# Self attention stage: one group of query-key products, operations moved off VectorE, input rows stored in halves, steps written out

## What is computed

```python
phi_q = relu(q) + 0.001;  phi_k = relu(k) + 0.001
kv  = cumsum(einsum('bshm,bshd->bshmd', phi_k, v), axis=1)
num = einsum('bshm,bshmd->bshd', phi_q, kv)
den = einsum('bshm,bshm->bsh', phi_q, cumsum(phi_k, axis=1))
attn = num / den[..., None]                       # 16 heads of 32
# block:  x1 = x + xattn(x);  u = layernorm(x1);  y = layernorm(u) * s1 + b1
#         q, k, v = y @ w_qkv;  xm = attn @ wo2 + u;  z = layernorm(xm) * s2 + b2
#         out = x1 + z + xm + gelu(z @ w1 + b1) @ w2 + b2
```

## Time and profile before

| what | value |
|---|---|
| median of 3 runs | 3508.2 us |
| profiled execution, first to last instruction | 3505.6 us |
| TensorE busy | 3440.8 us, 98% |
| VectorE busy | 1766.6 us, 50% |
| ScalarE busy | 1110.5 us, 32% |
| GpSimd busy | 2032.7 us, 58% |
| mean granted TensorE clock | 0.997 |
| self attention stage, `y` transposes of steps 2 to 16 | 2396.47 to 2690.32 us |

### The profile page before, as it was taken

How to read it: one execution, slowest core, us unless ns; L and a number is a source line. 1 busy time by engine, 2 the same in 40 slices (tenths; PEclk the granted TensorE clock), 3 DMA queues, 4 the chain that set the end, 5 groups by cost and what they waited for, 6 DMA issues and landing times.

```text
span 3505.6 us, 77874 instructions
## 1 busy us (share of the span) xinstructions
PE 3440.8 (98%) x32204; PEld 2683.7 (77%) x32204; DVE 1766.6 (50%) x3285; ACT 1110.5 (32%) x1284; POOL 2032.7 (58%) x1175
## 2 busy tenths in 40 slices
PE   7999999999999999999999999999999999999999
PEld 6777777777777777777777777777777788878887
DVE  6523333233332333333323333256888688789997
ACT  2233333333333333333333333342112422321111
POOL 3177867778677787786777867733444400123332
PEclk9999999999999999999999999999999999999999
DMA  4111110110110101111011011021112432320000
GB/s 139 58 43 35 37 35 31 41 47 28 38 40 25 47 28 44 34 37 35 29 44 36 35 35 45 27 89 41 49 51 78 136 99 99 126 67 25 24 18 19
DMA packets 83371, 174.64 MB, mean 50 GB/s; under 512 B 7184, under 2 KB 43152, under 8 KB 73872
## 3 DMA queue, kind: packets, MB, share of 16 engines
q1 hardware_dynamic: 83088, 170.24, 14.3%
HBM read 136.39 MB, written 33.82 MB: 49 GB/s over the span
## 4 chain that ended last, share of the span: by engine, by line
PE 89%; DVE 7%; issue 2%; ACT 1%; DMA 1%; POOL 1%; SPq 0%; DVEq 0%; ACTq 0%; POOLq 0%
PE a_bank L92 64%; PE a_bank L1294 8%; PE a_bank L1321 7%; PE a_bank L1309 6%; PE a_bank L1304 2%; DVE s_rden L604 1%; DVE s_am L546 1%; PE a_bank L2280 0%; PE a_bank L1340 0%; ACT x_probsT L1077 0%; DMA m_ff_src<-in_w_ff 0%; DVE m_hT L1753 0%; DVE s_yT L577 0%; PE a_bank L763 0%; DVE s_st L104 0%
## 5 line engine op out<-in xcount | busy, mean ns | idle before, releaser
L1155 DVE TENSOR_REDUCE x_maxima<-a_bank 128x1 f32<-128x512 f32 x960 | 593.4, 683 | 1226.1 <-PE a_bank L1294 1226.1
L92 PE MATMUL a_bank<-x_wv,x_ctx 128*128 128x512 f32 x3072 | 745.3, 396 | 1.1 <-ACT q_out L204 1.1
L894 POOL TENSOR_TENSOR x_pairs<-x_probsT 128x1024 f32<-128x1024 f32 x240 | 572.8, 2387 | 297.0 <-ACT x_probsT L1069 297.0
L92 PE MATMUL a_bank<-x_ctx,x_wk 128*128 128x512 f32 x3072 | 742.4, 396 | 0.0
L92 PEld LDWEIGHTS a_bank<-x_wv,x_ctx 128*128 128x128 f32 x3072 | 563.8, 188 | 166.5 <-DVE x_maxima L1155 27.3
L92 PEld LDWEIGHTS a_bank<-x_ctx,x_wk 128*128 128x128 f32 x3072 | 564.7, 188 | 135.7 <-issue 11.9
L1069 ACT ACTIVATE x_probsT<-a_bank 128x2048 f32<-128x2048 f32 x240 | 451.7, 1882 | 329.1 <-PE a_bank L1309 329.1
L1062 ACT ACTIVATE x_v<-a_bank 128x512 f32<-128x512 f32 x256 | 152.9, 597 | 611.8 <-PE a_bank L92 611.8
L1058 ACT ACTIVATE x_k<-a_bank,x_bk 128x512 f32<-128x512 f32 x256 | 176.2, 688 | 481.6 <-PE a_bank L92 481.6
L1002 POOL TENSOR_TENSOR x_ctx<-x_ctx_raw,x_ctx 128x2048 fp32r<-128x2048 f32 x64 | 294.7, 4604 | 5.0
L1294 PE MATMUL a_bank<-x_k,x_q_max 32*128 32x512 f32 x2048 | 283.5, 633 | 0.0
(11 more groups left out here) (207 smaller groups left out, 3987.1 us busy)
## 6 DMA issues: line engine op xcount, KB each, us to landing
x_ctx_raw<-in_ctx SPq DMA_DIRECT2D x64, 1024.0 KB, 5.0
m_ff_src<-in_w_ff SPq DMA_DIRECT2D x44, 192.0 KB, 2.5
wq_ff<-m_ff_dst SPq DMA_DIRECT2D x44, 192.0 KB, 1.8
m_w_raw<-in_w SPq DMA_DIRECT2D x32, 256.0 KB, 2.8
f_w_in<-wq_ff SPq DMA_DIRECT2D x22, 256.0 KB, 3.4
q_x<-in_x SPq DMA_DIRECT2D x16, 256.0 KB, 4.4
q_all<-q_out SPq DMA_DIRECT2D x16, 256.0 KB, 2.2
x_q_max<-q_all SPq DMA_DIRECT2D x16, 256.0 KB, 7.1
```

The costliest lines, as they stand in the source:

```text
L92: mm = pe.matmul(out, lhs[a], rhs[b], start=first and n == 0, stop=last and n == 2)
L894: eng.tensor_tensor(pairs[:], probs(i, s)[:, :, 0:2], probs(i, s)[:, :, 2:4], ALU.add).then_inc(paired, 1)
L1155: dve.tensor_reduce(maxima[:, c, g * HG + j:g * HG + j + 1], banks[:, j], AX.X, ALU.max).then_inc(maxed, 1)
```

## The change

- The query-key products of all four strips are issued in one call, at the place of the second call before, and masked by two operations of 1024 columns instead of four of 512.
- `attT` in device memory holds two halves. GpSimd makes them after the bias (two operations more per item), the store moves 512 KB and not 256, the stage loads them straight into the matmul's operand, and `input_hi` and `input_lo` are gone.
- `phi_q` and `kT` move from VectorE to ScalarE, where 0.001 is added after the transposition. The residual is computed on GpSimd as `xm + x1`; the sum `xu` is gone.
- Statistics are BN_STATS, BN_AGGR and one small addition.
- VectorE's list is reordered: reciprocal first, then the low half of `yT`, `an`, `x1`, the low half of `an`, `u`, the masks, `yn`, `xm` and `zn`.
- `normalise_last` and the bias behind it move from step 2 to the end of step 5, the store to step 6.
- All steps on all engines are written out; there is no hardware loop in the stage.

```diff
+STAT_LINKS = 2
+def row_stats(dve, src, st, eps, chain, before, var_ready):
+    dve.bn_stats(st[:, 0:6], src).then_inc(chain, 1)
+    dve.wait_ge(chain, before + 1)
+    dve.bn_aggr(st[:, 8:10], st[:, 0:6]).then_inc(chain, 1)
+    dve.wait_ge(chain, before + 2)
+    dve.tensor_scalar(st[:, 10:11], st[:, 9:10], eps, None, ALU.add).then_inc(var_ready, 1)
...
+def written_out(step, depth, first=0):
+    for n in range(first, B + depth):
+        step(Tile(n // UNROLL, n % UNROLL))
...
-        await_count(sp, attT_lo, s.count(plus=-1))
-        sp.dma_start(att_t[:, s.ring(2)], att_v[s.n][s.k]).then_inc(att_loaded[s.ring(2)], 16)
+        await_count(sp, m1, s.count(plus=-1))
+        sp.dma_start(attT[s.ring(2)][:].bitcast(F32), att_v[s.n][s.k]).then_inc(att_loaded[s.ring(2)], 16)
...
-            if nth(s, 2):
+            if s.count() == LAST_AT + 1:
...
-            if add_last_bias and nth(s, 2):
-                add_last_bias()
             rsqrt(pool, 0, s)
-            pool.wait_ge(u_ready, START + s.count(plus=1))
-            pool.tensor_tensor(xu[s.k][:], x1[:], u[s.k][:], ALU.add).then_inc(xu_ready, 1)
...
+            pool.wait_ge(xm_ready, START + e.count(plus=1))
+            await_count(pool, r_stored[e.ring(2)], e.back(e.ring(2)).count(8))
+            pool.tensor_tensor(r_out[:, e.ring(2)], xm[:], x1[e.k][:], ALU.add).then_inc(r_ready, 1)
...
+        if add_last_bias and s.count() == LAST_AT:
+            add_last_bias()
...
+            act.wait_ge(qkv, START + e.count(3, 1))
+            act.activation(phi_q[:], bank[0], ACT.Relu).then_inc(q_ready, 1)
...
-            act.activation(qT[:], bank[5], ACT.Copy).then_inc(qT_ready, 1)
-            if drain(s) == 0:
-                act.wait_ge(set_up, START + 4)
-                act.wait_ge(t3, START + e.count(2, 2))
-                act.activation(kT[:], bank[6], ACT.Identity, bias=eps_t[:]).then_inc(kT_ready, 1)
+            act.activation(qT[:], bank[5], ACT.Identity, bias=eps_t[:]).then_inc(qT_ready, 1)
+            act.wait_ge(t3, START + e.count(2, 2))
+            act.activation(kT[:], bank[6], ACT.Identity, bias=eps_t[:]).then_inc(kT_ready, 1)
...
+    def mask_products(dve, e):
+        dve.wait_ge(a_done, START + e.count(plus=1))
+        mask = causal[:].rearrange("p (g s) -> p g s", g=1).to_broadcast([P, 2 * DC, S])
+        for j in range(0, HG, 2):
+            dve.tensor_tensor(am[:, j:j + 2].rearrange("p j g s -> p (j g) s"),
+                              banks[:, 2 + j:4 + j].rearrange("p j (g s) -> p (j g) s", g=DC), mask,
+                              ALU.mult).then_inc(am_ready, 1)
...
+        await_count(dve, r_ready, e.count())
         dve.wait_ge(m3, START + e.count(plus=1))
         dve.tensor_tensor(xm[:], bank[2], u[e.k][:], ALU.add).then_inc(xm_ready, 1)
-        dve.wait_ge(xu_ready, START + e.count(plus=1))
-        await_count(dve, r_stored[e.ring(2)], e.back(e.ring(2)).count(8))
-        dve.tensor_tensor(r_out[:, e.ring(2)], bank[2], xu[e.k][:], ALU.add).then_inc(r_ready, 1)
...
+    def invert(dve, e):
+        dve.wait_ge(nd, START + e.count(plus=1))
+        dve.reciprocal(rden[:], bank[4]).then_inc(rden_ready, 1)
+    def scale_attention(dve, e):
+        dve.wait_ge(rden_ready, START + e.count(plus=1))
+        await_count(dve, anT_lo, e.count())
+        dve.tensor_tensor(an[:], bank[3], rden[:], ALU.mult).then_inc(an_ready, 1)
     def dve_step(dve, s, normalise_last=None):
-        e = s.back(1)
-        if e.exists() and not nth(e, 0):
-            turned_lo(dve, e)
-        e = s.back(3)
-        if e.exists():
-            dve.wait_ge(nd, START + e.count(plus=1))
-            dve.reciprocal(rden[:], bank[4]).then_inc(rden_ready, 1)
-            dve.wait_ge(rden_ready, START + e.count(plus=1))
-            await_count(dve, anT_lo, e.count())
-            dve.tensor_tensor(an[:], bank[3], rden[:], ALU.mult).then_inc(an_ready, 1)
-        if drain(s) == 1:
-            attention_lo(dve, e)
+        e1, e2, e3 = s.back(1), s.back(2), s.back(3)
+        if e3.exists():
+            invert(dve, e3)
+        if e1.exists() and not nth(e1, 0):
+            turned_lo(dve, e1)
+        if e3.exists():
+            scale_attention(dve, e3)
+        if s.exists():
+            add_input(dve, s)
         if drain(s) == 2:
             add_attention(dve, s.back(4))
-            attention_lo(dve, e)
+        if e3.exists():
+            attention_lo(dve, e3)
+        if drain(s) == 2:
             stage.after.hidden_lo(dve, 0, 0)
             output_norm(dve, s.back(4))
-        e = s.back(2)
-        if e.exists():
-            dve.wait_ge(set_up, START + 4)
-            mask_products(dve, e, 0)
-            mask_products(dve, e, 1)
-        if normalise_last and nth(s, 2):
+            stage.after.hidden_lo(dve, 0, 1)
+        if s.exists():
+            scale_input(dve, s)
+        if e2.exists():
+            if nth(e2, 0):
+                dve.wait_ge(set_up, START + 4)
+            mask_products(dve, e2)
+        if drain(s) == 1:
+            for j in range(MT):
+                stage.after.input_lo(dve, 0, j, stage.after.first_tr[j])
+        if s.exists():
+            normalise_input(dve, s)
+        if e3.exists() and drain(s) != 1:
+            add_attention(dve, e3)
+            output_norm(dve, e3)
+        if normalise_last and s.count() == LAST_AT:
             normalise_last()
-        e = s.back(3)
-        if e.exists() and drain(s) not in (1, 2):
-            attention_lo(dve, e)
-        if s.exists():
-            input_norm(dve, s)
-        e = s.back(1)
-        if e.exists():
-            dve.wait_ge(qkv, START + e.count(3, 1))
-            dve.tensor_scalar(phi_q[:], bank[0], 0.0, eps_k, ALU.max, ALU.add).then_inc(q_ready, 1)
-        if drain(s) == 1:
-            stage.after.input_lo(dve, 0, 0, stage.after.first_tr[0])
-        e = s.back(2)
-        if e.exists():
-            mask_products(dve, e, 2)
-            mask_products(dve, e, 3)
-        if drain(s) == 1:
-            for j in range(1, MT):
-                stage.after.input_lo(dve, 0, j, stage.after.first_tr[j])
-        if drain(s) == 2:
-            stage.after.hidden_lo(dve, 0, 1)
-        e = s.back(3)
-        if e.exists() and drain(s) != 1:
-            add_attention(dve, e)
-            output_norm(dve, e)
-        e = s.back(1)
-        if e.exists() and drain(s) != 0:
-            dve.wait_ge(t3, START + e.count(2, 2))
-            dve.tensor_scalar(kT[:], bank[6], eps_k, None, ALU.add).then_inc(kT_ready, 1)
...
-    def query_keys(pe, e, first):
+    def query_keys(pe, e):
+        pe.wait_ge(qT_ready, START + e.count(plus=1))
+        pe.wait_ge(kT_ready, START + e.count(plus=1))
+        await_count(pe, an_ready, e.count())
         for g in range(DC):
             cols = slice(g * P, (g + 1) * P)
-            for j in PRODUCT_ORDER[first:first + 2]:
+            for j in range(HG):
                 rows_j = slice(j * DH, (j + 1) * DH)
                 mm = pe.matmul(bank[3 + j][:, cols], kT[rows_j, cols], qT[rows_j, cols], start=True, stop=True)
-                if g == DC - 1:
-                    mm.then_inc(a_done, 1)
+        mm.then_inc(a_done, 1)
...
-        pe.wait_ge(attT_lo, START + s.count(plus=1))
-        await_count(pe, r_ready, s.back(3).count())
-        product(pe, bank[2], attT, 0, s, m1)
+        pe.wait_ge(att_loaded[s.ring(2)], START + s.back(s.ring(2)).count(8, 16))
+        await_count(pe, xm_ready, s.count(plus=-3))
+        product(pe, bank[2], [attT[s.ring(2)][:, k] for k in range(2)], 0, s, m1)
...
-            e = s.back(2)
-            if e.exists():
-                pe.wait_ge(qT_ready, START + e.count(plus=1))
-                pe.wait_ge(kT_ready, START + e.count(plus=1))
-                query_keys(pe, e, 0)
             if s.exists():
...
-                await_count(pe, an_ready, e.count())
-                query_keys(pe, e, 2)
+                query_keys(pe, e)
...
-                    await_count(pe, r_ready, e.count())
+                    await_count(pe, xm_ready, e.count())
...
-        pipeline(nc, pe, step, 3, first=2)
+        written_out(step, 3, first=2)
...
-                sp.wait_ge(out_ready, START + (i + 1))
-                sp.dma_start(attT[i], out_t[:]).then_inc(stored, 16)
+                sp.wait_ge(out_lo, START + (i + 1))
+                sp.dma_start(attT[i], out_hl[i is LAST][:].bitcast(F32)).then_inc(stored, 16)
...
+                hi, lo = (out_hl[i is LAST][:, k] for k in range(2))
+                pool.wait_ge(out_ready, START + (i + 1))
+                pool.tensor_tensor(hi, out_t[:], one[:].rearrange("p a b -> p (a b)").to_broadcast([P, D]),
+                                   ALU.mult).then_inc(out_hi, 1)
+                pool.wait_ge(out_hi, START + (i + 1))
+                pool.tensor_tensor(lo, out_t[:], hi.bitcast(F32), ALU.subtract).then_inc(out_lo, 1)
...
-                if s == 2:
-                    late.input_hi(act, FIRST)
-                if s == 7:
```

(25 more changed lines are left out.)

55 lines of the change are left out of this document (21 added, 34 removed).

## The result

Before 3508.63 us (3507.95 to 3509.17), after 3487.48 us (3485.56 to 3490.3), medians of four runs each: 21.1 us faster, ratio 0.9941 with an interval of 0.9929 to 0.9953. The forecast was 3488.9. The profiled execution of the changed kernel has a span of 3488.5 us and a time of 3490.3 us, 1.8 more and not 2.6 as I carried over; it is the slowest of its four, and in the two profiles the difference of the spans is 17.1 us.

A forecast was written before the change was run, and what follows sets the result against it. TensorE's own work sets the step, busy 177.79 of 185.31 us in steps 7 to 15. Stage gains of 18.8, 1.6, 2.1, 5.8 and 3.0 less 2.5, 2.3, 4.7 and 2.5 give 19.3 us, 3508.2 to 3488.9; range 3476 to 3502.

The forecast's parts named there:

- One group saves 1.25 us: Each stage step: one four-strip query-key group at 1.07 us replaces two groups taking 2.32 us a tile.
- The new race, 4.2 against 4.4 us: Steady step: yT's low half is ready at 4.2 us, TensorE's queries arrive at 4.4, so no wait, margin 0.2 us.
- VectorE and GpSimd as a loop, 17.4 us with 1.1 to spare: Steady step: the round from reciprocal through GpSimd to zn ends after 17.4 us, 1.1 us inside the 18.5 us step.
- Step 2 at 19.9: Stage step 2: queries wait 2.4 us for yT_lo behind the last weight; about 19.9 us, a gain of 3.0.
- Step 4: Stage step 4: ScalarE's 2.75 us pause at the hardware loop's entry goes; 24.27 to 18.5 us, a gain of 5.8.
- Step 6 at 23.1: Stage step 6: normalise_last at step 5's end delays the reciprocal 2.75 us; 23.1 us against 20.6, a loss of 2.5.
- Step 16, -2.3: Stage step 16: no input product covers the reciprocal, so queries wait about 2.7 us; a loss of 2.3 us.
- The border, -4.7: Border to the last item: GpSimd's halves (2.4 us) and a larger store (+1) delay the first weight; a loss of 4.7 us.
- The hand-over, -2.5 between 1.3 and 6.5: Stage's end into the MLP: r_out on GpSimd behind weight halves is done 5 us later; a loss of 2.5 us.
- the pauses don't arise: Rival, chance 0.15: no delays at steps 6 and 16 or from the weight's load; 9.5 us more won, 3479.
- the VectorE-GpSimd round: Rival, chance 0.13: this round sets the step at 19.45 us, costing 13 us over 14 steps, 3502.
- the starved engine: Rival, chance 0.05: straight-line code causes pauses of about 4.3 us each; with nine of them 3528 us, slower.

The follow-up runs named there:

- x1: Changed kernel with its query-key products in two groups again (strips 2 and 3, then 0 and 1): 3496.73 us, ratio 0.9969.
- x11: Changed kernel with kT made by VectorE again at the end of each step, ahead of the reciprocal: 3508.49 us, ratio 1.0.
- x2: Changed kernel with the seven-instruction statistics of the kernel before: 3489.04 us, ratio 0.9947.
- x3: Changed kernel with the load of the stage's first weight issued ahead of the store of the last item's halves: 3480.51 us, ratio 0.9919.
- x6: Changed kernel with yT's low half ahead of the reciprocal on VectorE in step 16 alone: 3487.97 us, ratio 0.9941.
- x8: Kernel before with its steps written out instead of looped, nothing else: 3505.68 us, ratio 0.9994.
- x5: Changed kernel with the last item's division (reciprocal and product) at the end of step 2 instead of step 5: 3484.64 us, ratio 0.9928.
- x7: Changed kernel with LAST_AT = 2 and a hardware loop over steps 4 to 15 on four engines, VectorE written out: 3486.01 us, ratio 0.9943.
- x9: Changed kernel with the edits of x3, x4 and x5 together: 3476.21 us, ratio 0.9908.
- x10: x9 plus yT's halves first on both engines in step 16 and MLP weight 5 loaded ahead of the last tile's stores: 3470.83 us, ratio 0.9892.
- x4: Changed kernel without TensorE's wait for r_ready ahead of the MLP's first output product: 3485.1 us, ratio 0.9935.

## Why the prediction held, point by point

- **TensorE sets the step; steps of 18.3 to 18.8 us.** Right: 18.40.
- **One group saves 1.25 us.** A little high, and the reason was half right: it saves 1.08 us from start to start. I priced it as strips side by side; x1 shows 0.55 us for that, and the rest for not going to 32-row work twice. The busy times that I took (2.32 a tile) count what overlaps the next product. The waits were worth more than their names said: 0.53 and 0.21 us are given, but from the `y` transposes to the next group it was 1.14 us and is 0.36, and the products behind the two groups came 0.40 us late. So 1.08 + 1.18 - 0.08 make up the 2.18 us of step 7, the 0.08 being slightly longer queries: the forecast was 0.17 too high on the merge and 0.44 too low on the waits. Four strips take 1.17 us busy here, not the 1.5 that I worked out from the Trainium skill's 3.07 times (TensorE: Matmul & The Clock Gate, Part 3). That figure is given for 512 columns and these products have 128, so the trace does not speak against the page, only against carrying it over.
- **The new race, 4.2 against 4.4 us.** Right, and the most useful line of the text: in the changed kernel `yT`'s low half is done 4.04 us after the feature transposes' start (2517.62 to 2521.66), and TensorE's queries start 0.09 us later, so the margin is 0.1 us and not 0.2. x11, which delays the reciprocal by 1.6 us, pays 1.61. I had not said that `kT`'s move off VectorE is what makes the race winnable; I had priced it as a wait of 0.53 us.
- **VectorE and GpSimd as a loop, 17.4 us with 1.1 to spare.** 2499.36 to 2516.16 is 16.8, and 1.59 is to spare. BN_AGGR is 0.18, against the 0.25 taken. x2 shows that the spare time takes 1.3 us more of work, and that only 0.86 us of it are used up, since `zn`'s wait for GpSimd gets shorter (1.85 us for 2.85).
- **Step 2 at 19.9.** The wait is right (2.53 for 2.4), the clock is not: none lost here, 1.6 us in x3. The failed term is "each pause of 2.5 to 3 us cost 1.6 to 2.6 us of slower matmuls" (the rows behind it give 1.6 and 2.4). The same pause costs nothing or 1.3 to 1.6 us, in code that is the same (x6).
- **Step 4.** Right as a gain (18.40 us), wrong as a reason: "without the loop that goes" is refuted by x8, where a pause of 1.73 us shows in step 5. In the changed kernel ScalarE shows none with "issue" in the stage. Why it doesn't, no run here tells.
- **Step 6 at 23.1.** 22.29: the wait is 2.11, since VectorE had 1.6 us free and not 1.2.
- **Step 16, -2.3.** The sum is right (the stretch lost 2.2; 3.7 us in x5, x7 and x9 with the same code there), the mechanism incomplete: ScalarE's weight halves cost as much as the reciprocal, as x6 and x10 show.
- **The border, -4.7.** Mis-sized: 6.7. GpSimd's 2.4 us were right (2.45); "+1 us is my guess" for the transfer was 2.7, and the clock fell for longer than I counted. Eight profiles with this border agree: 66.0 to 67.6 us for the last item, 59.8 to 60.3 in three of the old one. x3 shows that nothing else is late there.
- **The hand-over, -2.5 between 1.3 and 6.5.** 5.2 in the two profiles, 3.3 by the medians of the seven and the three profiles above: the forecast was too small, by how much is not resolved. I expected the time to be won back behind weights that pace TensorE; x4 shows that about half of it is (2.4 of 5.49 us are gained without the wait). I also took the wait for `r_out` as given, though the change had made it needless.

The forecast of the total was right in part by luck, since errors cancelled: in the two profiles the stage's steps gave 3.6 us more than forecast (32.4 for 28.8), the border and the hand-over 4.7 less, the scatter before the last item 1.2 less. Against the medians the forecast was 1.4 us off. Of the rivals, "the pauses don't arise" came true only for the clock in step 2; the VectorE-GpSimd round never set the step; four strips do overlap (x1); the starved engine did not show.

## What to carry to other kernels

When an engine gets shorter, look at what stands ahead of its late operation and not at its busy time: 1.3 us less of statistics were worth nothing in any steady step; one 0.69 us copy that had to wait for its input cost all 21 us when it went back ahead of the reciprocal, and in the old order its move bought nothing. After moving an operation, go through every semaphore that other engines still wait on for it, and through what the DMA queue has behind a store that grew. A named wait may have a second chain that ends just before it; ask for both before you move one.
